# An attention step in another order: probabilities times v ahead of v, scores ahead of the output projection, the output's transposes last

## What is computed

```python
q = rmsnorm(heads(x @ wq.T), q_norm_w); k = rmsnorm(heads(x @ wk.T), k_norm_w); v = heads(x @ wv.T)
q, k = apply_rope(q, cos, sin), apply_rope(k, cos, sin)
scores = 50.0 * tanh(einsum('bhtd,bhsd->bhts', q, k) * DH ** -0.5 / 50.0)
attn = softmax(where(mask, -inf, scores))
out = einsum('bhts,bhsd->bhtd', attn, v).transpose(0, 2, 1, 3).reshape(B, T, NH * DH) @ wo.T
```

```python
y = (exp(o - no) * p + exp(u + k - no) * v) / (exp(o - no) * q + exp(u + k - no))
```

## Time and profile before

| | us |
|---|---|
| median of 3 runs | 2114.24 (2112.72 to 2115.64) |
| the profiled execution | 2110.27, its span 2108.2 |
| attention stage, steps 0 to 127 | 52 to 1083 |
| TensorE busy | 2011.4 (95%) |
| VectorE, ScalarE, GpSimd busy | 1078.3, 937.0, 1033.7 |
| landing of xT (L944), median | 4.1 |

### The profile page before, as it was taken

The page is one execution under the profiler, slowest core; times in us unless marked ns, Lnnn a source line. Parts: engine busy times, 40 slices in busy tenths (PEclk is TensorE's granted clock), DMA queues, the critical chain, the costliest instruction groups (busy, mean ns, idle before and its releaser), DMA issues.

```text
span 2108.2 us, 41622 instructions
## 1 busy us (share of the span) xinstructions
PE 2011.4 (95%) x12200; PEld 1816.6 (86%) x12201; DVE 1078.3 (51%) x2350; ACT 937.0 (44%) x2127; POOL 1033.7 (49%) x1077
## 2 busy tenths in 40 slices
PE   3999999999999999999978999899999999999998
PEld 2888888888888888888868899899999999999997
DVE  5555555555677767667666636433333333333332
ACT  5455545554565656556555411233333333233232
POOL 3444434442355544444547403667644222388885
PEclk9999999999999999999998999999999999999999
DMA  8877767777877777774525324767645343499899
GB/s 309 294 251 247 250 227 252 251 248 253 298 263 291 251 288 257 267 257 175 211 83 196 107 92 166 253 210 253 208 134 155 122 124 123 123 212 217 196 214 240
DMA packets 189240, 451.53 MB, mean 214 GB/s; under 512 B 21696, under 2 KB 21952, under 8 KB 189120
## 3 DMA queue, kind: packets, MB, share of 16 engines
q1 hardware_dynamic: 135648, 339.73, 47.4%
q0 software_dynamic: 21504, 51.13, 10.4%
q10 hardware_dynamic: 31968, 59.12, 8.7%
HBM read 276.41 MB, written 173.48 MB: 213 GB/s over the span
## 4 chain that ended last, share of the span: by engine, by line
PE 86%; POOL 4%; issue 3%; ACT 3%; DVE 2%; DMA 1%; SPq 0%; ACTq 0%; POOLq 0%
PE bank L1207 20%; PE bank L1081 15%; PE bank L1217 11%; PE bank L1125 7%; PE bank L1099 7%; PE bank L178 5%; PE bank L727 5%; PE bank L1146 3%; PE bank L1111 3%; PE bank L737 3%; PE bank L744 2%; PE bank L1138 1%; POOL ex L1427 1%; PE bank L475 1%; DMA xT<-xT_att 1%
## 5 line engine op out<-in xcount | busy, mean ns | idle before, releaser
L1207 PE MATMUL bank<-w_hi,xT 128*128 x1776 | 473.7, 329 | 3.0 <-DVE xT L1644 2.6
L1081 PE MATMUL bank<-w_hi,xT 128*128 128x512 f32 x1024 | 353.4, 407 | 14.4 <-DMA xT<-xT_att 10.4
L1413 POOL TENSOR_TENSOR rr<-rr,expo 128x4 f32<-128x4 f32 x128 | 128.9, 1007 | 416.5 <-DVE rr L1532 416.5
L1207 PEld LDWEIGHTS bank<-w_hi,xT 128*128 128x128 f32 x1776 | 316.1, 189 | 10.9 <-issue 5.7
L754 DVE TENSOR_TENSOR hT<-bank,hT 128x384 fp32r<-128x384 f32 x143 | 79.7, 558 | 477.1 <-ACT hT L751 477.1
L1207 PE MATMUL bank<-w_lo,xT 128*128 x888 | 286.5, 323 | 0.0
L1081 PEld LDWEIGHTS bank<-w_hi,xT 128*128 128x128 f32 x1024 | 197.3, 193 | 54.7 <-issue 13.9
L1217 PE MATMUL bank<-w_hi,hT 128*128 x666 | 228.7, 397 | 2.1 <-DVE hT L754 2.0
L1099 PE MATMUL bank<-w_hi,xT 128*128 128x256 f32 x1024 | 213.8, 292 | 0.0
L751 ACT ACTIVATE hT<-bank 128x384 fp32r<-128x384 f32 x143 | 70.1, 490 | 321.1 <-PE bank L744 316.0
L1081 PE MATMUL bank<-w_lo,xT 128*128 128x512 f32 x512 | 203.7, 398 | 0.0
(11 more groups left out here) (228 smaller groups left out, 4487.7 us busy)
## 6 DMA issues: line engine op xcount, KB each, us to landing
xT<-xT_att SPq DMA_DIRECT2D x128, 512.0 KB, 4.1
w_hi<-w_split SPq DMA_DIRECT2D x64, 512.0 KB, 6.5
w_lo<-w_split SPq DMA_DIRECT2D x64, 512.0 KB, 7.3
xg<-blank SPq DMA_DIRECT2D x111, 264.0 KB, 4.3
yg<-blank SPq DMA_DIRECT2D x111, 256.0 KB, 4.5
raw<-in_weights SPq DMA_DIRECT2D x88, 272.0 KB, 3.0
w_split<-w_hi SPq DMA_DIRECT2D x64, 272.0 KB, 3.3
w_split<-w_lo SPq DMA_DIRECT2D x64, 272.0 KB, 3.5
```

Source lines behind the costliest of these rows:

```text
L1081: last = pe.matmul(bank[par][:, :], xT[:, par, a, c * P:(c + 1) * P], w_hl[w][:, fw, c * 512:(c + 1) * 512], start=n == 0, stop=n == 11)
L1207: last = pe.matmul(out_[:, 0:I], xT[:, par, a, c * P:(c + 1) * P], flat(w_hl[w])[:, bass.ds(at + (c * 2 * I + half_ * I), I)], start=n == ...
L1413: pool.tensor_tensor(rr[:, :], rr[:, :], expo[:, :], ALU.pow).then_inc(pw_done, 1)
```

## The change

TensorE's step is put in the order: q and k, transposes of `rot`, PV, v, recurrence "mid", scores, output projection, transposes of `on`, recurrence "end". On ScalarE `oT` high goes behind exp. On VectorE the division (`rden`, `on`) goes ahead of `vE` low, and `rec_dve` goes behind `pT` low. GpSimd and SP keep their order. No instruction is added or taken away, and each keeps its waits.

```diff
--- before.py
+++ after.py
@@ -1088,6 +1088,17 @@
                         pe.wait_ge(k_out, s)
                         pe.wait_ge(rot_done, 2 * s)
                         transposes(pe, QT_, lambda c: rot[:, c * P:(c + 1) * P], t_done)
+                    if back:
+
+                        pe.wait_ge(p_hi, s - 1)
+                        pe.wait_ge(p_lo, s - 1)
+                        pe.wait_ge(v_hi, s - 1)
+                        pe.wait_ge(v_lo, s - 1)
+                        for h in range(HG):
+                            for n, (a, w) in enumerate(TERMS):
+                                last = pe.matmul(O_[:, h * 130:(h + 1) * 130], pT[:, a, h, :],
+                                                 vE[:, (at4 - 2) % 4, w, h, :], start=n == 0, stop=n == 2)
+                        last.then_inc(pv_done, 1)
                     if front:
                         wait(pe, v_hi, s)
                         wait(pe, v_lo, s)
@@ -1100,19 +1111,17 @@
                                                  w_hl[w][:, fw, at:at + 256], start=n == 0, stop=n == 11)
                                 n += 1
                         last.then_inc(v_done, 1)
-                    if back:
-
-                        pe.wait_ge(p_hi, s - 1)
-                        pe.wait_ge(p_lo, s - 1)
-                        pe.wait_ge(v_hi, s - 1)
-                        pe.wait_ge(v_lo, s - 1)
+                    if rec:
+                        rec_pe(pe, s - SPLIT, "mid")
+                    if mid:
+                        pe.wait_ge(qkT_hi, s)
+                        pe.wait_ge(qkT_lo, s)
+                        wait(pe, th_done, 2 * s - 2)
                         for h in range(HG):
                             for n, (a, w) in enumerate(TERMS):
-                                last = pe.matmul(O_[:, h * 130:(h + 1) * 130], pT[:, a, h, :],
-                                                 vE[:, (at4 - 2) % 4, w, h, :], start=n == 0, stop=n == 2)
-                        last.then_inc(pv_done, 1)
-                    if rec:
-                        rec_pe(pe, s - SPLIT, "mid")
+                                last = pe.matmul(S_[:, h * T:(h + 1) * T], qkT[:, a, (HG + h) * T:(HG + h + 1) * T],
+                                                 qkT[:, w, h * T:(h + 1) * T], start=n == 0, stop=n == 2)
+                        last.then_inc(s_done, 1)
                     if tail:
                         pe.wait_ge(oT_hi, s - 2)
                         pe.wait_ge(oT_lo, s - 2)
@@ -1137,15 +1146,6 @@
                         for h in range(HG):
                             last = pe.transpose(OT_[:, h * T:(h + 1) * T], on[:, h * DH:(h + 1) * DH], ident[:, :])
                         last.then_inc(ot_done, 1)
-                    if mid:
-                        pe.wait_ge(qkT_hi, s)
-                        pe.wait_ge(qkT_lo, s)
-                        wait(pe, th_done, 2 * s - 2)
-                        for h in range(HG):
-                            for n, (a, w) in enumerate(TERMS):
-                                last = pe.matmul(S_[:, h * T:(h + 1) * T], qkT[:, a, (HG + h) * T:(HG + h + 1) * T],
-                                                 qkT[:, w, h * T:(h + 1) * T], start=n == 0, stop=n == 2)
-                        last.then_inc(s_done, 1)
                     if rec:
                         rec_pe(pe, s - SPLIT, "end")
                 attention(pe, step)
@@ -1282,9 +1282,6 @@
                         act.activation(vE[:, at4, 0, :, 0:DH], heads(V_[:, 0:256]), ACT.Copy).then_inc(v_hi, 1)
                     if rec:
                         rec_act(act, s - SPLIT, "first")
-                    if back:
-                        act.wait_ge(ot_done, s - 1)
-                        act.activation(oT[:, 0, :, :], heads(OT_[:, 0:256]), ACT.Copy).then_inc(oT_hi, 1)
                     if mid:
                         act.wait_ge(s_done, s)
                         act.wait_ge(rms_done, s)
@@ -1294,6 +1291,9 @@
                         act.wait_ge(th_done, 2 * s)
                         wait(act, p_lo, s - 1)
                         act.activation(ex, th, ACT.Exp, scale=CAP).then_inc(ex_done, 1)
+                    if back:
+                        act.wait_ge(ot_done, s - 1)
+                        act.activation(oT[:, 0, :, :], heads(OT_[:, 0:256]), ACT.Copy).then_inc(oT_hi, 1)
                     if mid:
                         act.wait_ge(mask_done, s)
 
@@ -1531,9 +1531,6 @@
                         dve.wait_ge(ss_done, s + 1)
                         dve.tensor_scalar(rr[:, :], ssq[:, :], 1.0 / DH, RMS_EPS, ALU.mult, ALU.add)\
                             .then_inc(ms_done, 1)
-                        dve.wait_ge(v_hi, s + 1)
-                        dve.tensor_tensor(vE[:, at4, 1, :, 0:DH], heads(V_[:, 0:256]),
-                                          vE[:, at4, 0, :, 0:DH].bitcast(F32), ALU.subtract).then_inc(v_lo, 1)
                     if back:
                         dve.wait_ge(pv_done, s - 1)
                         av = O_[:, 0:HG * 130].rearrange("p (h n) -> p h n", h=HG)
@@ -1542,6 +1539,10 @@
                         dve.tensor_tensor(heads(on), av[:, :, 0:DH],
                                           rden[:, :].unsqueeze(2).to_broadcast([P, HG, DH]),
                                           ALU.mult).then_inc(on_done, 1)
+                    if front:
+                        dve.wait_ge(v_hi, s + 1)
+                        dve.tensor_tensor(vE[:, at4, 1, :, 0:DH], heads(V_[:, 0:256]),
+                                          vE[:, at4, 0, :, 0:DH].bitcast(F32), ALU.subtract).then_inc(v_lo, 1)
                     if front:
                         dve.wait_ge(pw_done, s + 1)
                         dve.wait_ge(k_out, s + 1)
@@ -1558,12 +1559,12 @@
                         dve.wait_ge(oT_hi, s - 1)
                         dve.tensor_tensor(oT[:, 1, :, :], heads(OT_[:, 0:256]), oT[:, 0, :, :].bitcast(F32),
                                           ALU.subtract).then_inc(oT_lo, 1)
-                    if rec:
-                        rec_dve(dve, s - SPLIT)
                     if mid:
                         dve.wait_ge(p_hi, s)
                         dve.tensor_tensor(pT[:, 1, :, :], heads(ex), pT[:, 0, :, :].bitcast(F32),
                                           ALU.subtract).then_inc(p_lo, 1)
+                    if rec:
+                        rec_dve(dve, s - SPLIT)
```

## The result

| | us |
|---|---|
| before, median of 4 runs | 2113.48 (2111.47 to 2115.64) |
| after, median of 4 runs | 2134.53 (2129.39 to 2139.58) |
| ratio, 95% interval | 1.0104 (1.0081 to 1.0126) |
| the profiled execution after | 2137.17, its span 2135.1 |

Slower by 21.0 us in the medians, by 26.9 in the spans of the two profiled executions. The forecast was 2145 within 2120 to 2172.

The account below looks back on a forecast made before the run. TensorE, busy 95% of the span, was taken as the bound. Slots +23.7, last steps +2.5 and clock +5 made +31.2 us: 2141.5 for a profiled execution, 2145 for the median, range 2120 to 2172.

Parts of the forecast that it names:

- Plain steps: Attention steps without heavy recurrence work: they stay at 7.6 us, a margin of 0.3 us at the scores sufficing; +0.
- The slots: Second-half steps, numbered by place in the 11-step recurrence period: TensorE idle 41.7 us after against 18.0 before, +23.7.
- r=9: Second-half step at place 9 of the 11-step recurrence period: scores wait 0.5 us, against 0 before.
- r=6: Second-half step at place 6 of the 11-step recurrence period: scores wait 2.95 us, against 1.07 before.
- Last steps: Steps 124 to 127, which waited 6 us before: 2.5 us more, between 0 and 5.
- Clock: TensorE's granted clock after long idle stretches: four falls at 1.3 us, +5, between 0 and +15.
- Queues: SP's fetch of xT, waiting for a later V: 0, between -2 and +2 us; weight pieces keep their places.
- Two moves have a price here: Second half: scores issued 1.6 us earlier relative to their inputs, and `rec_dve` behind `pT` low, cost time; net +23.7.
- Faster: Rival: TensorE's two waits go and scores wait only for the square, if `pT` low ends by +1.5; 2101, chance 0.09.
- No change: Rival: waits merely move, `rec_dve` fits, the square is as late as before; 2114 give or take 4, chance 0.06.
- Plain steps lose: Rival: the scores' 0.3 us margin fails, costing 0.1 to 0.2 in 120 steps; 2157 to 2169, chance 0.08.
- Much slower: Rival: each long wait drops the clock, the scan keeps 3.22, PV's margin is used up; 2168 to 2185, chance 0.09.

Follow-up runs that it names:

- the repetition: The changed kernel, nothing altered, measured once more against the kernel before: 2136.26 us, ratio 1.0121.
- R: The kernel before with only `rec_dve` moved behind `pT` low on VectorE: 2138.48 us, ratio 1.0161.
- P: The kernel before with only PV moved ahead of v and the division ahead of `vE` low: 2123.63 us, ratio 1.0067.
- S: The kernel before with only scores ahead of the projection, `oT` high behind exp, transposes of `on` last: 2101.83 us, ratio 0.9969.
- S, R: The kernel before with scores ahead of the projection and `rec_dve` behind `pT` low, PV still behind v: 2128.25 us, ratio 1.0079.

## Why the prediction was right, and where it wasn't

**Plain steps, +0.** Right: 7.58 to 7.59, with 0.43 us to spare at the scores.

**The slots, +23.7; measured +20.6** (38.5 after, 17.9 before, for 41.7 and 18.0). The mechanism is as described, step by step: `pT` low at +2.8, the scan at 2.30, the table load ahead of its wait, the scores 0.1 behind `qkT` low. Each slot is right to 0.25 us, and all but r=9 are a bit too high, r=6 because `pT` low ended at +2.84 where I took +3.1. The load at 918.11 starts 0.02 behind `pT` high (917.67 + 0.42); the drain of 1.38 us that the Trainium skill names (ScalarE: Activation LUTs, What ACT_TABLE_LOAD costs) isn't in this trace either, and the 2147 that it would have given was the wrong way.

**Last steps, +2.5; measured +3.7. Clock, +5; measured +3.3**: five stretches at 1.5 to 1.7 us each, 8.0 in all, against three before, 4.7. I had added four falls at 1.3 and taken none away, though the kernel before had three. The two mistakes work against each other, so it is luck that the term came out no further off; in the repetition there were seven. In the changed kernel's first profile the granted clock was 1.00 in the wait of step 103, and 0.68 and 0.80 in the two stretches after it:

```profile
884.90:888.10 3.20, 0.74 (x7) 0.56 (x6) 3.17 (x11) 1.28 (x3) 0.00 (x0) 1.00 1.05 329
888.10:891.30 3.20, 3.20 (x15) 2.60 (x15) 1.44 (x6) 1.04 (x3) 3.02 (x3) 0.68 0.94 335
891.30:894.70 3.40, 3.40 (x14) 2.78 (x13) 1.49 (x3) 1.71 (x4) 1.85 (x4) 0.80 1.03 422
```

Step 81 of the same profile has the same wait, with as many matmuls in the 3.2 us around it, and the clock stayed at 1.00 behind it:

```profile
686.20:689.40 3.20, 0.74 (x7) 0.56 (x6) 3.17 (x11) 1.28 (x3) 0.00 (x0) 1.00 0.84 236
689.40:692.80 3.40, 3.40 (x19) 2.91 (x20) 2.44 (x7) 1.43 (x4) 3.23 (x3) 1.00 0.62 235
```

**Queues, 0; measured -2.2**: the one wait for xT went, and with it the low clock of step 96, counted above.

**From the profiled execution to the median, +4.** This is the larger miss. The forecast for a profiled execution was 2141.5, and it was 2137.2. I then added 4 because the profiled run of before lay 4 under its median; that of after lay 2.6 above its own. Of the 10.5 us between 2145 and 2134.5 this step makes 6.1 (3.5 added, 2.6 not there). The offset was no property of the kernel.

**The step that failed is "Two moves have a price here".** The sum was right since it followed the waits of the new order as a whole; how it was shared out was wrong.
- *Scores earlier* has no price but a gain: 0.9969 alone, and 1.0079 against 1.0161 where `rec_dve` is behind. I asked only when the scores want their operand and not what an earlier tanh and exp release: the mask where it waits for exp, and with it `pT` high, ScalarE's queue and the next squares.
- *PV earlier*, which I called covered, costs 0.7% alone and 0.2 to 0.4% in the change. That it has a cover of 0.1 us at all it owes to R, which takes `rec_dve` from ahead of `pT` low; what it still costs then comes at least in part by v's end, which delays `vE` high and ScalarE's queue by 0.6 to 0.7. I had listed SP as the one that waits for v and overlooked ScalarE, whose recurrence operations stand behind `vE` high.
- *`rec_dve` behind `pT` low* is the loss: 1.6% alone.

**The rivals.** *Faster* named as its condition `pT` low by about +1.5, by a mask ahead of GpSimd's operation, and a time, 2101. With the mask there the kernel took 2156.8, and `pT` low ended at +3.76 in r=6, so the mask's place doesn't bring what the rival needs. *No change* and *Plain steps lose* did not happen. *Much slower* did not happen either: the scan kept 2.30, and PV's margin held. `pT` low ended at +3.09 at the latest in the slots with a GpSimd operation, and PV waited in the last steps only (4.3 us, twice). Without R it has no margin, as P alone shows.

**The marks named in advance.** No wait for `on` at its transposes; 38.5 us of waits in the slots, for 41.7; the mask at 0.72 to 0.75 in all 128 steps and the scan at 2.30 in seven of eight (2.72 once), where the earlier trace rows had 3.22 as the median:

```profile
L640 DVE TENSOR_TENSOR_SCAN qS<-a,e x8: 2301/2302/2720, 593.4 to 1207.4; 128x1032 f32<-128x1032 f32 x8
```

```profile
L1427 POOL TENSOR_TENSOR ex<-ex,mask x128: 715/737/751, 65.4 to 1117.5; 128x256 f32<-128x256 f32 x128
```

**What stays open.** Which waits of 2 to 3 us drop the clock was not settled: in the same kernel the same wait of 2.7 us did in one period and not in another. And the gain of S is larger with R (0.8%) than alone (0.3%): the waits of a period fell by only 0.5 us (8.1 to 7.6), some 2.3 in all; part of the rest is such stretches, eight in the profile of R alone and six in that of S, R, and how much was not measured.

## What to carry to other kernels

When an engine's queue is reordered, work out for each moved piece both what it now waits for and what its end sets free or holds up on every other engine; the second gave the gain of the scores' move and the hidden cost of PV's. Put the long work of a side job ahead of a short operation only if the short one's reader has the slack for it, and behind it only if nothing on the critical path stands behind both: here `rec_dve` was best left ahead, beside a reader (PV) that stays late. A change made of several moves can hide a good one among bad ones, so run the moves one by one: 0.997, 1.007 and 1.016 were in this one, and the good one alone with a halved scan gave 0.995.

## What was not expected of the hardware

- An instruction of 0.43 us on VectorE (`pT` low, two inputs) took 2.15 when it started 0.5 us into a GpSimd operation of 2.40, and ended 0.28 behind it; a mask of 0.74 on GpSimd took 2.75 beside VectorE's scan. In both pairs the one that started first kept its own length (2.40; 2.37 for a scan of 2.30), so the order of starts, 0.15 us apart in step 103 of the scores' move, decides which of the queues is delayed by 2 us.
- ScalarE's table load ran at 918.11 although the operation that needs it waited until 920.32, so its 1.28 us were hidden in that wait.
- After a wait of 2.3 us at PV the granted clock was 0.50 over 3.4 us (885.60 to 889.00, PV alone moved), the 1.2 GHz level; after the 2.5 us ahead of the scores in step 81 of the changed kernel it was 1.00 over as long.
